# Two scatters of an expert block issued together, with spare rows of their own, and attention started one slot earlier

## The reference

```python
x = x + tanh(g_xattn[0]) * attention0(layernorm(x), ctx)   # 16 heads of 16
x = x + tanh(g_ffn[0])   * experts0(layernorm(x))          # 8 experts + a shared one, computed densely
x = x + tanh(g_xattn[1]) * attention1(layernorm(x), ctx)   # logits clipped to +-10000
x = x + tanh(g_ffn[1])   * experts1(layernorm(x))          # 8 experts, the best 2 of each row
```

## Time and profile before

| | us |
|---|---|
| median of 3 runs | 1143.86 (1134.05 to 1147.37) |
| the profiled execution | 1147.23 |
| its span in the trace | 1145.5 |
| PE busy | 959.5 (84%) |
| DVE busy | 767.7 (67%) |
| ACT busy | 481.4 (42%) |
| POOL busy | 244.7 (21%) |

### The profile page before, as it was taken

How to read it: one execution, slowest core, us unless ns; L and a number is a source line. 1 busy time by engine, 2 the same in 40 slices (tenths; PEclk the granted TensorE clock), 3 DMA queues, 4 the chain that set the end, 5 groups by cost and what they waited for, 6 DMA issues and landing times.

```text
span 1145.5 us, 18008 instructions
## 1 busy us (share of the span) xinstructions
PE 959.5 (84%) x6385; PEld 757.2 (66%) x6385; DVE 767.7 (67%) x1608; ACT 481.4 (42%) x834; POOL 244.7 (21%) x388
## 2 busy tenths in 40 slices
PE   3478999999999989889897678973699799797992
PEld 2355667777776756666564355542599799797992
DVE  2544667677667586786866678856488588586770
ACT  1124534444444333333233233431476466464660
POOL 2011111010110010101000022110434444444633
PEclk9656999999999999899897676565699899898997
DMA  4996735145245162643527544322656666567542
GB/s 110 230 201 118 141 68 101 47 65 94 54 76 77 48 111 76 107 120 96 104 87 143 132 100 117 108 71 94 232 163 197 184 190 212 157 213 229 143 113 27
DMA packets 122057, 141.89 MB, mean 124 GB/s; under 512 B 11537, under 2 KB 106409, under 8 KB 121969
## 3 DMA queue, kind: packets, MB, share of 16 engines
q1 hardware_dynamic: 113136, 128.50, 44.9%
q0 software_dynamic: 8832, 12.25, 5.6%
HBM read 109.97 MB, written 30.75 MB: 123 GB/s over the span
## 4 chain that ended last, share of the span: by engine, by line
PE 38%; DVE 17%; issue 15%; DMA 15%; POOL 8%; ACT 4%; SPq 2%; POOLq 0%; DVEq 0%; ACTq 0%
DMA out_x<-x,token_i 10%; PE bank L765 8%; POOL out_x L1737 5%; PE bank L775 4%; DVE clipped L1261 3%; DVE rowmax L1236 3%; PE by_query L673 3%; PE bank L659 3%; PE bank L620 3%; PE value_bank L709 3%; PE bank L736 3%; PE by_key L694 2%; POOL xs_in L1724 2%; DMA lower<-max 2%; PE bank L629 2%
## 5 line engine op out<-in xcount | busy, mean ns | idle before, releaser
L1236 DVE TENSOR_REDUCE rowmax<-by_query 128x4 f32<-128x1024 f32 x128 | 155.7, 1216 | 25.1 <-PE by_query L673 25.0
L1051 ACT ACTIVATE probs<-clipped 128x1024 f32<-128x1024 f32 x64 | 67.6, 1057 | 185.1 <-DVE clipped L1261 185.0
L1737 POOL DMA_INDIRECT out_x<-x,token_i x46 | 97.0, 2110 | 167.8 <-DMA out_x<-x,token_i 142.3
L1686 POOL TENSOR_SCALAR rstd<-moments 128x2 f32<-128x2 f32 x32 | 7.1, 223 | 575.3 <-DVE moments L1200 575.3
L926 PE MATMUL bank<-w_hi,h_hi 128*128 128x256 f32 x368 | 104.1, 283 | 0.0
L926 PE MATMUL bank<-w_lo,h_hi 128*128 128x256 f32 x368 | 104.1, 283 | 0.0
L926 PE MATMUL bank<-w_hi,h_lo 128*128 128x256 f32 x368 | 104.1, 283 | 0.0
L673 PE MATMUL by_query<-stack_k,stack_q 48*128 48x256 f32 x512 | 72.4, 365 | 35.0 <-DVE rowmax L1236 30.1
L673 PEld LDWEIGHTS by_query<-stack_k,stack_q 48*128 48x128 f32 x512 | 43.9, 212 | 77.7 <-issue 39.3
L1261 DVE SCALAR_TENSOR_TENSOR clipped<-by_key,lower 128x512 f32<-128x512 f32 x128 | 82.0, 682 | 9.4 <-DMA lower<-max 7.0
L694 PE MATMUL by_key<-stack_q,stack_k 50*128 50x256 f32 x512 | 69.2, 353 | 20.2 <-DVE clipped L1261 18.5
(11 more groups left out here) (237 smaller groups left out, 2250.1 us busy)
## 6 DMA issues: line engine op xcount, KB each, us to landing
w<-in_L_ffn_W SPq DMA_DIRECT2D x46, 1024.0 KB, 6.5
lower<-max SPq DMA_DIRECT2D x64, 256.0 KB, 3.5
stack_k<-qk SPq DMA_DIRECT2D x96, 128.0 KB, 4.8
stack_q<-qk SPq DMA_DIRECT2D x96, 128.0 KB, 7.4
qk<-hi SPq DMA_DIRECT2D x32, 256.0 KB, 4.1
qk<-lo SPq DMA_DIRECT2D x32, 256.0 KB, 5.3
rows<-w_gate SPq DMA_DIRECT2D x8, 264.0 KB, 4.0
x<-in_x SPq DMA_DIRECT2D x8, 256.0 KB, 7.4
```

Of the source, the lines that this page charges most:

```text
L1051: ac.activation(probs[i % 4][:, :, :, :].rearrange("p h k s -> p (h k s)"), src, ACT.Exp).then_inc(sem.exp_done, 1)
L1236: dv.tensor_reduce(rowmax[u % 2][:, 2 * p:2 * p + 2, :], by_query[:, :, :].rearrange("p h (t s) -> p h t s", t=TT), AX, ALU.max).then_inc( ...
L1737: po.indirect_dma_start(out[:, :], bass.IndirectOffsetOnAxis(ap=token_i[:, n:n + 1].bitcast(U32), axis=0), ysb[i % 3][:, t, :], None, comp ...
```

## The change

Five things are changed.

1. The spare rows become 256 (`BT * P`), one set for each of a block's two scatters (`spare_row` has a column for each). The two scatters of a block are then issued one right behind the other, and POOL waits for `added` once for each block, ahead of the first.
2. The stand-in rows of all batches come in one DMA (`load_alternative`, 128 x 2048), 20 half slots before the last unit. `reload` is left for batches 0 to 3 only, 9 half slots ahead of its `pick_z` instead of 6, and waits for less.
3. In the last layer block 0's `up` and `hidden` come before block 1's `turn_rows` and `split_rows` and before the splits of block 0's W2 and block 1's W1.
4. The wait that the output with the biases is stored (`x_out`) moves from the start of the last layer on four engines to ACT's first `hidden`.
5. `LAG` goes from 11 to 10.

```diff
-LAG = 11
+LAG = 10
...
+    at[g - 20].append(("load_alternative", 0))
...
-        at[g - 6].append(("reload", b))
+        if b < KEPT_FROM:
+            at[g - 9].append(("reload", b))
...
-    xn1_dram = nc.dram_tensor("rows1", (NB * S + P, WIDE), F32).ap()
+    xn1_dram = nc.dram_tensor("rows1", (NB * S + BT * P, WIDE), F32).ap()
...
-    spare_row = sb("spare_row", [P, 1])
+    spare_row = sb("spare_row", [P, BT])
...
-    alt_row = [in_place_of(w_down0, i, D)[:, 0, :] for i in range(4)]
+    alt_rows = w_down0[:, 0:NB, :]
...
-        engine.wait_ge(sem.x_out, 16 * NB)
-        engine.wait_ge(sem.pad_out, 32)
+        engine.wait_ge(sem.pad_out, 32 * BT)
...
-            sp.dma_start(xn1_dram[NB * S:NB * S + P, :], zero_row[:, :]).then_inc(sem.pad_out, 16)
-            sp.dma_start(out[NB * S:NB * S + P, :], zero_row[:, 0:D]).then_inc(sem.pad_out, 16)
+            for t in range(BT):
+                spare = slice(NB * S + t * P, NB * S + t * P + P)
+                sp.dma_start(xn1_dram[spare, :], zero_row[:, :]).then_inc(sem.pad_out, 16)
+                sp.dma_start(out[spare, :], zero_row[:, 0:D]).then_inc(sem.pad_out, 16)
...
+        def load_alternative(_):
+            sp.wait_ge(sem.zalt_out, 16)
+            sp.wait_ge(sem.y_done, N0 * NB)
+            sp.dma_start(alt_rows.rearrange("p b d -> p (b d)"),
+                         zalt_dram.rearrange("b d -> (b d)").partition_broadcast(P)).then_inc(sem.zalt_in, 16)
...
         def reload(b):
-            sp.wait_ge(sem.zalt_out, 16)
-            sp.wait_ge(sem.y_done, N0 * NB)
-            if b >= 4:
-                sp.wait_ge(sem.x_final, b - 3)
-            if b < KEPT_FROM:
-                sp.wait_ge(sem.z_out, 16 * (b + 1))
-                sp.dma_start(z_rows[b % 4], z_dram[b].rearrange("(t p) d -> p t d", p=P)).then_inc(z_in[b % 4], 16)
-            sp.dma_start(alt_row[b % 4], zalt_dram[b].partition_broadcast(P)).then_inc(z_in[b % 4], 16)
+            sp.wait_ge(sem.z_out, 16 * (b + 1))
+            sp.wait_ge(sem.gu_done, N0 * NB)
+            sp.dma_start(z_rows[b], z_dram[b].rearrange("(t p) d -> p t d", p=P)).then_inc(z_in[b], 16)
...
         turn_rows(0)
+        up(0)
         turn_rows(1)
-        up(0)
...
             if i == 0:
                 ac.wait_ge(sem.b1_ready, 1)
+                ac.wait_ge(sem.x_out, 16 * NB)
...
         split_w1(0)
         split_rows(0)
+        hidden(0)
         split_rows(1)
         split_w2(0)
         split_w1(1)
-        hidden(0)
...
-        table(dv.tensor_scalar(tok[:, 0, :], down_bank[0][:, COLS:2 * COLS], 0.0, spare_row[:, 0:1], ALU.is_equal, ALU.mult))
+        for t in range(BT):
+            table(dv.tensor_scalar(tok[:, 0, :].rearrange("p (i t) -> p i t", t=BT)[:, :, t],
+                                   down_bank[0][:, COLS:2 * COLS].rearrange("p (i t) -> p i t", t=BT)[:, :, t], 0.0,
+                                   spare_row[:, t:t + 1], ALU.is_equal, ALU.mult))
...
             po.wait_ge(sem.y_ready, i + 1)
+            if i:
+                po.wait_ge(sem.added, 16 * BT * i)
             for t in range(BT):
                 n = BT * i + t
-                if n:
-                    po.wait_ge(sem.added, 16 * n)
                 po.indirect_dma_start(out[:, :], bass.IndirectOffsetOnAxis(
```

More of the change, by code:

```diff
@@ L153 @@
 gate_turned gate_wT_ready routed0 sig_exp route_chain cw_ready gu_done tanh_done half_done h_ready y_done x_acc
-flag_chain flag_ready flag_mm keep_ready zalt_ready zalt_out
+flag_chain flag_ready flag_mm keep_ready zalt_ready zalt_out zalt_in
 z_in0 z_in1 z_in2 z_in3 z_picked x_final biasT_mm biasT_ready bias1_mm x_done x_out logits_mm logits_ready mask_ready soft_ready exp1_done counted
@@ L185, in share_banks @@
             if stage in ("load", "stack", "stats", "normal", "take", "groups0", "ranks0", "weights0", "any_nan",
-                         "reload", "pick_z", "soft1", "count1", "weights1", "tables") or (stage == "ctx" and layer_of(n)):
+                         "reload", "load_alternative", "pick_z", "soft1", "count1", "weights1", "tables") or (stage == "ctx" and layer_of(n)):
                 continue
@@ L569, in _ @@
         stages = {"load": load, "ctx": context, "kprod": store_keys, "qprod": store_queries, "stack": load_stacks,
-                  "shift_turn": place_shift, "mean_project": store_alternative, "project": store_z, "reload": reload,
+                  "shift_turn": place_shift, "mean_project": store_alternative, "project": store_z, "reload": reload, "load_alternative": load_alternative,
                   "weights1": store_rows, "bias1": store_x, "tables": first_weights}
@@ L1412, in pick_z @@
             dv.wait_ge(sem.keep_ready, 2)
-            dv.wait_ge(z_in[b % 4], 32 if b < KEPT_FROM else 48)
-            if b >= KEPT_FROM:
+            dv.wait_ge(sem.zalt_in, 16)
+            if b < KEPT_FROM:
+                dv.wait_ge(z_in[b], 16)
+            else:
                 dv.wait_ge(sem.z_ready, b + 1)
             for t in range(TT):
-                op = dv.copy_predicated(z_rows[b % 4][:, t, :], keep_row[:, 0:1].broadcast_to([P, D]), alt_row[b % 4])
+                op = dv.copy_predicated(z_rows[b % 4][:, t, :], keep_row[:, 0:1].broadcast_to([P, D]), alt_rows[:, b, :])
             op.then_inc(sem.z_picked, 1)
@@ L1665, in _ @@
             (part_no[:, :], [[0, 1]], 0, 1),
-            (spare_row[:, :], [[0, 1]], NB * S + 1, 1),
+            (spare_row[:, :], [[P, BT]], NB * S + 1, 1),
             (tile_start[:, :], [[0, TOPK1], [P, NT]], 0, 0),
@@ L1754 @@
         aps[name] = nc.dram_tensor(f"in_{name}", v.shape, mybir.dt.from_np(v.dtype), kind="ExternalInput").ap()
-    out = nc.dram_tensor("out_x", (NB * S + P, D), F32, kind="ExternalOutput").ap()
+    out = nc.dram_tensor("out_x", (NB * S + BT * P, D), F32, kind="ExternalOutput").ap()
     build(nc, aps, out)
```

## The result

The changed kernel takes **1092.26 us** (median of 4 executions, 1089.51 to 1095.50) against 1144.43 of the kernel before in the same comparison: the ratio is 0.9565, 95% interval 0.9508 to 0.9621. The profiled execution took 1095.50 us, its span is 1093.4. Forecast were 1098 and a range of 1086 to 1118.

A forecast was written before the change was run, and what follows sets the result against it. The prediction took POOL's serial scatters (13.3 us a block against PE's 11.95), late gathers and the attention list as bounds. It summed 1147.2 - 29.6 - 10.6 + 1.5 - 8 - 2 = 1098.5, stated as 1098 us, range 1086 to 1118.

The forecast's parts named there:

- pair: stalls and end: Last layer's scatters: 8 to 10 us a pair, no late gathers (-29.6 us), earlier end after the last block (-10.6).
- first block first: Start of last layer: block 0's `up` sooner, then a 7 us PE gap and half clock; +1.5 us, bounds -4 to +3.
- x_out: Start of last layer: gathers about 2 us sooner, covered by W1's low part; 0 us, at most +1.
- stand-ins, reloads: Attention stretch: 10.4 us of waits before `pick_z` go, part returns at lower-bound loads; -8 us, bounds -10.4 to +5.
- LAG 10: Attention list: slots of 3.4 and 4.0 us go, one of 5.38 comes; -2 us, bounds -7.4 to +8.
- Each sign named beforehand: Blocks: steps of 11.95 us, no PE wait for gathered rows, POOL waiting for ACT, end 10 us after last result.
- the first rival: Last layer's scatters: two together no quicker than one after another, 13.3 us; total 1137 us, chance 0.06.
- `up(1)` starts when it starts today: Start of last layer: block 1's `up` still starts at 826 us, since weight splits queue behind block 0's `hidden`.
- Rival 2: Blocks gain, attention does not: removed DVE waits return or the stretch grows; 1108 to 1120 us, chance 0.25.
- The counting of slots: Attention list one slot shorter: 3.4 and 4.0 us removed, 5.38 added, giving -2.0 us.
- rival 3: Attention stretch gains 5 to 12 us more, as fewer waits may raise the granted clock; 1086 to 1093 us, chance 0.09.

The follow-up runs named there:

- the fastest: The changed kernel with the old order of the first blocks (block 1's rows turned and split before block 0's `up` and `hidden`): 1083.29 us, ratio 0.9490.

## Why the prediction held, and where it did not

| term | forecast | measured | from |
|---|---|---|---|
| pair: stalls and end | -40.2 | -38.7, -39.7 | alone; all but it |
| first block first | +1.5 | +9.0 | change less the old order |
| x_out | 0 | -7.1 | taken out of the fastest |
| stand-ins, reloads | -8 | -6.3, -1.9 | alone; taken out of the fastest |
| LAG 10 | -2 | -9.1, -9.1, -9.0 | alone; LAG 11 in two kernels |
| sum | -48.7 | -49 with the last of each (whole change: -52.2) | |

The terms measured singly leave 3 to 4 us of the whole unassigned; they come from several comparisons, and a median here is uncertain by a few us.

**Pairs and the end: right, in mechanism and size.** Each sign named beforehand came: steps of 11.95, no wait for gathered rows, POOL's waits naming ACT, the last result 10.54 us ahead of the end (10.3 were worked out). The end also weighs the first rival, that a pair is no quicker than two scatters. Beside lightly loaded DMA engines (share 0.31 from 1077 to 1084) the last pair but one let the next go 6.4 us after its first issue. The last scatters of the kernel before, at a share of 0.28, came 4.1 us one after the other, 8.3 for two. Beside the weight loads, a pair takes the 9.5 estimated above against 13.3 for two scatters in turn. So the two overlap, but not wholly: with two in flight the median from issue to landing is 7.5 us, with one 5.8 (kernel before) and 4.6 (all but the pair). The first rival's 13.3 us a pair is what the prediction made, by a strict reading, of the Trainium skill's rule in "DMA: Bandwidth & Descriptors", "Rules for kernel authors", that two transfers to disjoint partition halves serialize. This trace does not agree with that reading for two scatters that each read all 128 partitions: no step of blocks 0 to 20 is above 11.97.

**First block first: the step that failed.** The gap was forecast at 7 us, and is 6.94; it is followed by the clock at 0.50, as forecast. What was wrong is the sentence ahead of it, "`up(1)` starts when it starts today". It took today's start of `up(1)`, 21 us after the first gather, as a fixed point and held it against the new order. But that start was late because block 1's rows were (PE waits 7.29 us for them, until 817.69), and the change moves those as well. In the old order with `x_out` moved, `up(1)` starts 17.1 us after the first gather; in the changed kernel it does 23.1 us after. So the order was charged at 1.5 and cost 9.0. In the two traces it is 8.6 from the first gather to block 0's end: 6.0 of later start, and 2.7 more from there, where the clock begins at half. I had costed one edit against a trace that did not have the other.

**x_out: the same mistake from the other side.** I wrote that gathers start about 2 us sooner, which W1's low part covers. They do start 1.3 us sooner (`token_i` to gather 1.17 instead of 2.49 in the pair of kernels above), and in the changed kernel block 0's `up` does wait for its rows' low part, which stands behind W1's on DVE. But the 1.3 us let the third and the fourth gather pass before DVE's subtraction is under way. Block 1's last gather is thereby issued 4.1 us after the first instead of 6.2, ahead of 2 MB of weights instead of behind, and its rows are turned, counted from the first gather, 5.9 us sooner (6.9 instead of 12.8). I had priced the wait against block 0 alone and at nothing. In the changed kernel block 1's rows come early too, but its `up` starts late all the same; no run puts the wait back there, so what it is worth in that order is open.

**Stand-ins: right that the waits go, wrong in what is left.** I charged half of one clip's 4.40. In the fastest kernel with and without this part, 5.1 go and 4.5 come back: nearly all. And there were only 5.1 to go: LAG 10 alone had already brought the 10.4 of the earlier trace rows down to 6.0, so that two terms of the sum claimed the same wait. A likely reason for what comes back is the order of SP's queue, where the one transfer of 1 MB and the earlier reloads stand among the loads of lower bounds that DVE needs next; no run moves them apart. Rival 2 said this, with "the removed waits on DVE come back"; it held for this part and not for LAG.

**LAG 10: mis-sized, and not by a slot.** The counting of slots gave 2 us. One reading under it was wrong: the scores by key at 82.64 did not wait for the maxima, as the rows under the result show, and they do start sooner with LAG 10, by 1.5 us in the changed kernel. To see what gave 9, compare the whole stretch from 45 us to `token_i` in the kernel before, the changed one, and the fastest with LAG 10 and with LAG 11 (one line of each kernel's windows, columns as in the earlier trace rows; the last line is the run with the `x_out` wait back, whose list of slots is that of the fastest kernel):

```profile
45.00:802.25 757.25, 657.12 (x4032) 460.97 (x4033) 524.04 (x1285) 280.96 (x512) 82.65 (x255) 0.84 0.47 102
```

```profile
45.00:786.94 741.94, 642.97 (x4033) 453.57 (x4033) 523.02 (x1286) 280.01 (x512) 82.78 (x255) 0.87 0.48 104
```

```profile
45.00:783.92 738.92, 645.90 (x4033) 454.56 (x4033) 523.01 (x1285) 280.03 (x512) 82.40 (x255) 0.86 0.48 105
```

```profile
45.00:792.41 747.41, 655.97 (x4033) 460.60 (x4033) 523.70 (x1285) 280.94 (x512) 82.58 (x255) 0.85 0.47 103
```

```profile
45.00:782.20 737.20, 634.92 (x4033) 448.95 (x4031) 522.73 (x1285) 280.22 (x512) 83.12 (x255) 0.88 0.48 105
```

PE's idle time is length less busy time: 100.1, 99.0, 93.0 and 91.4 us in the first four. It hardly differs between the two distances. What differs is how long the same 4033 matmuls take: 657.1 and 656.0 us with LAG 11, 643.0 and 645.9 with LAG 10, at a mean granted clock of 0.84 to 0.85 and 0.86 to 0.87. The other kernels agree (LAG 11: 654.5 and 656.0; LAG 10: 634.9 to 646.9; LAG 9: 642.4), but for the stand-ins alone, with LAG 11 and 644.1 in its one profiled execution, the fastest of its ten. The mean clock of every whole execution, not only of the profiled ones, says the same: 0.880 to 0.885 with LAG 11 against 0.891 to 0.897 in the changed kernel, 0.882 to 0.889 against 0.891 to 0.900 with the old order.

So the gain lies in the time of the matmuls and goes with the clock, which is what rival 3 pointed at. That the clock is its cause is not shown. The last line above warns of it: with the same list as the fastest kernel PE is busy 11.0 us less, at 0.88, but idle 9.3 us more, and the stretch is only 1.7 us shorter. Why one slot less goes with a higher clock I can't say from these runs. It comes bit by bit between 82 and 750 us, and no run fixes one of its causes; this is open.

The total came out within 6 us because the misses, +7.5, -7.1, +6.1 and -7, cancel, and that is luck: only the pair, three quarters of the gain, was priced within a microsecond or two. Of the 6 us, 2.8 are the distance of the profiled execution that the sum began from to the median.

## What to carry to other kernels

Price the parts of a change against each other's trace, not each against the trace of before: a moment that one edit takes as fixed may be late for a reason that another edit removes. Where a chain of read-add-write transfers has to stay in order, find out what must be apart (here only the spare rows of empty places collided) and let the rest be in flight together; look for the engine that falls behind by 1.4 us a block, since its cost shows elsewhere and later. Where a wait is moved, look at what else runs while the work behind it is issued: 1.3 us decided here which gathers met DVE's long subtraction. And where two orders of the same work differ by a few idle microseconds of TensorE, count the clock after them too.

## What the runs showed of the hardware that I had not expected

- With two indirect scatter-adds of 128 rows in flight the span ends 7.8 us after the second's issue began, with one alone 7.6; beside the weight loads the median from issue to landing is 7.5 us with two in flight, 5.8 and 4.6 with one.
- The issue of a gather on POOL took 3.04 us, and in another run 1.89, where DVE had begun 0.08 us, and 1.26 us, earlier to subtract 128 x 2048 numbers, and 0.95 in its neighbours; it ended 0.82 to 0.83 us after the subtraction.
- With PE busy for 200.00 of 200 us the granted clock stayed at 1.00 (2.4 GHz), with the DMA engines at a share of 0.72 and 225 GB/s.
- An idle time of 2.03 us on PE (W1 split ahead) already brought the clock down, from 1.00 in the 2.5 us ahead of it to 0.58 in the 3 us behind; 6.94 us brought 0.50 for the 3 us from 812 and 0.77 for the next five; 1.00 us in the fastest kernel left it at 1.00:

```profile
808.00:811.00 3.00, 3.00 (x19) 3.00 (x18) 2.90 (x3) 1.40 (x4) 0.00 (x0) 0.58 0.01 3
```

- A gather issued 1.2 us behind the start of two loads of 1 MB, on another queue, was followed by a wait of PE of 7.33 us; the same gather issued 1 us ahead of them, by one of 1.41.
- The stretch of the blocks repeats to 0.01 us from kernel to kernel (256.29 or 256.30 in all that have the pair), while the list of slots ahead of it, at a granted clock of 0.84 to 0.88, differs by 7 us between two kernels in which that list is the same (`token_i` at 799.41 and 792.41 in the two with LAG 11 put back).
